# Linear attention and FFN in one kernel: VectorE's prefix sums at the head of the slot, two of GpSimd's steps later, one order of TensorE's last products

## What is computed

```python
q = jnp.exp(split_heads(x @ Wq.T + bq))
k = jnp.exp(split_heads(x @ Wk.T + bk))
v = split_heads(x @ Wv.T + bv)
kv = jnp.cumsum(k[:, :, :, None] * v[:, :, None, :], axis=1)
k1 = jnp.cumsum(k, axis=1)
num = jnp.einsum('zsD,zsDd->zsd', q, kv)
den = jnp.sum(q * k1, axis=-1, keepdims=True)
x = layernorm(x + merge_heads(num / den) @ Wo.T + bo)
h = ((x @ weight) @ aux_weight1) @ aux_weight2
out = layernorm(x + jnp.tanh(h + bias))
```

## Time and profile before

| | |
|---|---|
| median of 3 runs | 2473.36 us |
| the profiled execution | 2476.86 us, span 2473.6 |
| TensorE matmuls | 2267.6 us, 92% of the span |
| TensorE weight loads | 1844.8 us, 75% |
| VectorE | 1935.6 us, 78% |
| GpSimd | 1432.5 us, 58% |
| ScalarE | 990.4 us, 40% |
| granted clock of TensorE, mean | 0.983 |

### The profile page before, as it was taken

One profiled execution on the slowest core, in us unless ns is written; L12 is line 12 of the kernel. 1 busy time (PEld: TensorE's weight loads), 2 busy tenths in 40 slices (PEclk: granted clock), 3 DMA queues, 4 the chain that ended last, 5 costly groups with the idle time before them and its releaser, 6 DMA issues.

```text
span 2473.6 us, 71230 instructions
## 1 busy us (share of the span) xinstructions
PE 2267.6 (92%) x27784; PEld 1844.8 (75%) x27784; DVE 1935.6 (78%) x2316; ACT 990.4 (40%) x1683; POOL 1432.5 (58%) x1925
## 2 busy tenths in 40 slices
PE   4999999999999999999999999999999999999863
PEld 3777777777787777777777777777778777777752
DVE  2578888888888888888888888888888888787753
ACT  2344434444344443444444434444344443443421
POOL 1265666656666566665666656666666666565642
PEclk9999999999999999999999999999999999999987
DMA  6133333333333333332333323333333333332211
GB/s 159 45 104 96 111 95 106 104 100 108 95 108 104 99 104 99 105 107 95 107 100 103 104 95 108 102 102 105 95 105 106 103 104 95 103 106 85 70 44 38
DMA packets 294452, 242.73 MB, mean 98 GB/s; under 512 B 33328, under 2 KB 225840, under 8 KB 294192
## 3 DMA queue, kind: packets, MB, share of 16 engines
q1 hardware_dynamic: 294192, 238.69, 31.2%
HBM read 139.99 MB, written 98.57 MB: 96 GB/s over the span
## 4 chain that ended last, share of the span: by engine, by line
DVE 40%; SPq 17%; issue 13%; DMA 9%; PE 8%; POOL 8%; ACT 5%; POOLq 0%; DVEq 0%; ACTq 0%
DVE WK L689 21%; DMA WK<-x_rows 7%; SPq L277 7%; SPq L284 6%; DVE o L677 4%; DVE k L694 4%; DVE bnst L704 4%; DVE xres L702 3%; ACT WK L524 3%; POOL rstd L770 3%; PE SC L312 2%; SPq L271 2%; PE SC L313 2%; PE SC L314 2%; POOL WK L725 2%
## 5 line engine op out<-in xcount | busy, mean ns | idle before, releaser
L689 DVE TENSOR_TENSOR_SCAN WK<-ones,k,KT 128x128 f32<-128x128 f32 x512 | 557.2, 1147 | 0.0
L677 DVE RECIPROCAL o<-ND 128x512 f32<-128x512 f32 x128 | 428.6, 3348 | 10.7 <-PE ND L419 10.7
L524 ACT ACTIVATE WK<-xres,shift,rstd 128x512 f32<-128x512 f32 x128 | 104.2, 814 | 812.8 <-POOL shift L772 812.8
L745 POOL TENSOR_TENSOR oL<-o,oH 128x512 fp32r<-128x512 f32 x128 | 168.7, 1318 | 274.9 <-ACT oH L544 274.9
L664 DVE BATCH_NORM_STATS2 bnst<-WK 128x6 f32<-128x512 f32 x128 | 88.9, 694 | 299.3 <-POOL WK L725 299.3
L729 POOL TENSOR_SCALAR_AFFINE_SELECT A<-A 128x512 f32<-128x512 f32 x512 | 309.6, 642 | 6.7 <-ACT A L534 6.7
L725 POOL TENSOR_TENSOR WK<-WK 128x512 f32<-128x512 f32 x128 | 163.7, 1279 | 191.3 <-ACT WK L529 191.3
L534 ACT ACTIVATE A<-SC 128x512 f32<-128x512 f32 x512 | 261.8, 594 | 11.8 <-PE SC L410 11.5
L312 PE MATMUL SC<-xTH,WqH 128*128 128x512 f32 x512 | 211.6, 413 | 56.7 <-ACT A L534 28.9
L312 PE MATMUL SC<-WfH,x1H 128*128 128x512 f32 x512 | 205.3, 401 | 45.9 <-POOL x1L L750 24.6
L767 POOL TENSOR_SCALAR ve<-mv 128x1 f32<-128x1 f32 x128 | 28.6, 223 | 351.0 <-DVE mv L706 350.9
(11 more groups left out here) (100 smaller groups left out, 5356.6 us busy)
## 6 DMA issues: line engine op xcount, KB each, us to landing
xin<-x SPq DMA_DIRECT2D x512, 64.0 KB, 2.0
xres<-x SPq DMA_DIRECT2D x128, 256.0 KB, 2.7
x_rows<-WK SPq DMA_DIRECT2D x128, 256.0 KB, 2.3
WK<-x_rows SPq DMA_DIRECT2D x512, 64.0 KB, 2.0
out<-WK SPq DMA_DIRECT2D x128, 256.0 KB, 2.0
k_rows<-WK SPq DMA_DIRECT2D x120, 256.0 KB, 2.5
WK<-k_rows SPq DMA_DIRECT2D x480, 64.0 KB, 1.9
QT<-wqT SPq DMA_DIRECT2D x4, 256.0 KB, 4.7
```

Source lines behind the costliest of these rows:

```text
L524: nc.scalar.activation(x1[:, n % 2, :], xres[:, n % 2, :], ACT.Identity, bias=shift[:, 0:1], scale=rstd[:, 0:1]).then_inc(x1_ready, 1)
L677: nc.vector.reciprocal(o[:, :, :], den_ps).then_inc(recip_ready, 1)
L689: last = nc.vector.tensor_tensor_scan(qk1[:, g, :], ones[:, 0:1].to_broadcast([P, P]), KT[:, s, g, cols], k1[:, k % B, g:g + 1], ALU.mult, ...
```

## The change

VectorE: the four prefix sums, the copy and the product with q (L689 to L697) move from behind the x1s transpose to directly behind L650. The statistics of the second layernorm (L664, L667) move from ahead of the state sum to behind o. GpSimd: the tanh sum (L725) moves from ahead of the masks to behind them; oL (L745) moves from behind the three one-element steps of the second layernorm to ahead of them. TensorE: the FFN is called behind the output projection in every slot, also from 124 on. Nothing is added or taken away; every wait moves with its instruction.

```diff
--- before.py
+++ after.py
@@ -459,11 +459,9 @@
                     wait(pe, scores_out[2], c.count(k + 1))
                     three_pass(v_ps, lambda f: xTH[:, s, f, cols], lambda f: xTL[:, s, f, cols],
                                lambda f: WvH[:, f, :], lambda f: WvL[:, f, :]).then_inc(v_done, 1)
-                if ffn and not proj:
-                    feed_forward()
                 if prev:
                     output_projection()
-                if ffn and proj:
+                if ffn:
                     feed_forward()
 
             run_slots(pe, slot, 8, 2, {-3: multiply_aux, -2: multiply_weight, -1: multiply_bv})
@@ -648,39 +646,6 @@
                     wait(dve, ffn_done, c.count(k - 2))
                     wait(dve, out_stored[(k - 5) % B], c.dma_count(k - 5))
                     nc.vector.tensor_tensor(yf, ffn_ps, bfbc[:, :], ALU.add).then_inc(z_ready, 1)
-                if c.updates_state(k - 1):
-                    wait(dve, k_ready, c.quad_count(k - 1))
-                    wait(dve, ktok_loaded[(k - 2) % B], c.part_count(k - 2))
-                    nc.vector.transpose(KS[:, :].rearrange("p (t g f) -> p g t f", t=HG, f=HD),
-                                        KT[:, ps, :, pcols].rearrange("p g (t q) -> p g t q", q=HD)
-                                        ).then_inc(k_turned, 1)
-                if c.exists(k + 8):
-                    m = k + 8
-                    wait(dve, xin_loaded[m % B], c.part_count(m))
-                    xblocks = xin[:, m % XIN, :]
-                    nc.vector.transpose(xblocks, xblocks).then_inc(x_turned, 1)
-                if fin:
-                    wait(dve, y_ready, c.count(k - 2))
-                    nc.vector.bn_stats(bnst[:, 1, :], yf).then_inc(bn2_ready, 1)
-
-                    wait_before(dve, (bn2_ready, c.count(k - 2)), (shift2_ready, c.count(k - 3)))
-                    nc.vector.bn_aggr(mv2[:, :], bnst[:, 1, :]).then_inc(stats2_ready, 1)
-                if c.updates_state(k - 2):
-                    wait(dve, state_done, c.count(k - 1))
-                    sflat = state[:, (k - 2) % B, :, :].rearrange("p g d -> p (g d)")
-                    nc.vector.tensor_tensor(sflat, state_ps, sflat, ALU.add).then_inc(state_ready, 1)
-                if prev:
-
-                    wait(dve, num_done, c.count(k))
-                    wait(dve, oh_ready, c.count(k - 1))
-                    wait(dve, ol_ready, c.count(k - 1))
-                    nc.vector.reciprocal(o[:, :, :], den_ps).then_inc(recip_ready, 1)
-                    wait(dve, recip_ready, c.count(k))
-                    nc.vector.tensor_tensor(o[:, :, :], num_ps, o[:, :, :], ALU.mult).then_inc(o_ready, 1)
-                if c.exists(k - 2):
-                    n = k - 2
-                    wait(dve, x1s_loaded[n % B], c.part_count(n))
-                    nc.vector.transpose(x1s[:, :], x1s[:, :]).then_inc(x1_turned, 1)
                 if att:
                     wait(dve, k_ready, c.quad_count(k))
                     wait(dve, den_done, c.count(k))
@@ -696,6 +661,39 @@
                     wait(dve, q_ready, c.quad_count(k))
                     nc.vector.tensor_tensor(qk1[:, :, :], qk1[:, :, :], QT[:, s, :, cols],
                                             ALU.mult).then_inc(qk1_ready, 1)
+                if c.updates_state(k - 1):
+                    wait(dve, k_ready, c.quad_count(k - 1))
+                    wait(dve, ktok_loaded[(k - 2) % B], c.part_count(k - 2))
+                    nc.vector.transpose(KS[:, :].rearrange("p (t g f) -> p g t f", t=HG, f=HD),
+                                        KT[:, ps, :, pcols].rearrange("p g (t q) -> p g t q", q=HD)
+                                        ).then_inc(k_turned, 1)
+                if c.exists(k + 8):
+                    m = k + 8
+                    wait(dve, xin_loaded[m % B], c.part_count(m))
+                    xblocks = xin[:, m % XIN, :]
+                    nc.vector.transpose(xblocks, xblocks).then_inc(x_turned, 1)
+                if c.updates_state(k - 2):
+                    wait(dve, state_done, c.count(k - 1))
+                    sflat = state[:, (k - 2) % B, :, :].rearrange("p g d -> p (g d)")
+                    nc.vector.tensor_tensor(sflat, state_ps, sflat, ALU.add).then_inc(state_ready, 1)
+                if prev:
+
+                    wait(dve, num_done, c.count(k))
+                    wait(dve, oh_ready, c.count(k - 1))
+                    wait(dve, ol_ready, c.count(k - 1))
+                    nc.vector.reciprocal(o[:, :, :], den_ps).then_inc(recip_ready, 1)
+                    wait(dve, recip_ready, c.count(k))
+                    nc.vector.tensor_tensor(o[:, :, :], num_ps, o[:, :, :], ALU.mult).then_inc(o_ready, 1)
+                if fin:
+                    wait(dve, y_ready, c.count(k - 2))
+                    nc.vector.bn_stats(bnst[:, 1, :], yf).then_inc(bn2_ready, 1)
+
+                    wait_before(dve, (bn2_ready, c.count(k - 2)), (shift2_ready, c.count(k - 3)))
+                    nc.vector.bn_aggr(mv2[:, :], bnst[:, 1, :]).then_inc(stats2_ready, 1)
+                if c.exists(k - 2):
+                    n = k - 2
+                    wait(dve, x1s_loaded[n % B], c.part_count(n))
+                    nc.vector.transpose(x1s[:, :], x1s[:, :]).then_inc(x1_turned, 1)
                 if prev:
                     wait(dve, oproj_done, c.count(k))
                     wait(dve, xb_ready, c.count(k))
@@ -719,10 +717,6 @@
                 ffn = c.exists(k - 2)
                 fin = c.exists(k - 3)
 
-                if fin:
-                    n = k - 3
-                    wait(pool, tanh_ready, c.count(n + 1))
-                    nc.gpsimd.tensor_tensor(y[:, n % 2, :], y[:, n % 2, :], x1[:, n % 2, :], ALU.add).then_inc(y_ready, 1)
                 if att:
                     for j in range(HG):
                         wait_before(pool, (scores_out[j], c.count(k + 1)))
@@ -730,6 +724,15 @@
                                                        compare_op=ALU.is_ge, fill=0.0, base=0,
                                                        pattern=[[0, NK], [1, P]], channel_multiplier=-1)
                     last.then_inc(masked, 1)
+                if fin:
+                    n = k - 3
+                    wait(pool, tanh_ready, c.count(n + 1))
+                    nc.gpsimd.tensor_tensor(y[:, n % 2, :], y[:, n % 2, :], x1[:, n % 2, :], ALU.add).then_inc(y_ready, 1)
+                if prev:
+                    wait(pool, oh_ready, c.count(k))
+                    wait(pool, oproj_done, c.count(k - 1))
+                    nc.gpsimd.tensor_tensor(oL[:, :, :], o[:, :, :], oH[:, :, :].bitcast(F32),
+                                            ALU.subtract).then_inc(ol_ready, 1)
                 if fin:
                     wait_before(pool, (stats2_ready, c.count(k - 2)))
                     nc.gpsimd.tensor_scalar(ve[:, 1:2], mv2[:, 1:2], EPS, None, ALU.add).then_inc(ve2_ready, 1)
@@ -739,11 +742,6 @@
                     wait_before(pool, (rstd2_ready, c.count(k - 2)))
                     nc.gpsimd.tensor_scalar(shift[:, 1:2], mv2[:, 0:1], rstd[:, 1:2], -1.0, ALU.mult,
                                             ALU.mult).then_inc(shift2_ready, 1)
-                if prev:
-                    wait(pool, oh_ready, c.count(k))
-                    wait(pool, oproj_done, c.count(k - 1))
-                    nc.gpsimd.tensor_tensor(oL[:, :, :], o[:, :, :], oH[:, :, :].bitcast(F32),
-                                            ALU.subtract).then_inc(ol_ready, 1)
                 if ffn:
                     wait(pool, x1h_ready, c.count(k - 1))
                     halves = [t[:, :, :].rearrange("p g (t q) -> p g t q", q=HD) for t in (x1H, x1L)]
```

## The result

After the change the kernel takes 2340.24 us, the median of 4 runs (2339.22 to 2341.11); the kernel before took 2473.22 in the runs beside them (4 runs, 2471.76 to 2480.55). The ratio is 0.9457, with a 95% interval of 0.9438 to 0.9476. The profiled execution took 2341.11 us, span 2339.2, mean granted clock 0.991.

The account below looks back on a forecast made before the run. TensorE's 17.24 us of work a slot plus 0.98 waiting for VectorE, whose scans GpSimd holds. 2476.9 - 98.0 (steady slots) - 20.9 (last slots) - 9.8 (last r) = 2348.2; median 3.5 lower: 2345, range 2318 to 2408.

Parts of the forecast that it names:

- (1): Prefix sums at VectorE's slot head: stage 2.41, reciprocal at 4.6, oL at 9.4, slack before Wo about 1.0 us.
- The price per us: Steady slots: each us of delay beyond the slack before Wo costs 119 us in all.
- (2): VectorE behind o: r no longer queues behind scans, L650 waits only for TensorE, at 0.11; both TensorE waits go.
- (3): SyncE's queue: k_rows store 0.26 later, at about 3.95; x1L ready at 14.0, slack 0.4 before Wf.
- (4): GpSimd's reordered list: tanh-sum waiting vanishes but not as time; xres and xTL to about 16.7, shift at about 0.6.
- (5): Last slots, Wo ahead of Wf: four slots 66 us, -20.9 (-25.7 to -15.3); last r at 13, -9.8.
- The head: Start of the kernel: has its setup and no such wait, so 0 us change.
- (D): Rival for the steady slots: TensorE's wait isn't VectorE's doing, only the tail gains; 2442 us, chance 0.06.
- (B): Rival at shift or x1L: shift meets the scans, or DMA delays x1L; slot 17.9, 2405 us, chance 0.17.
- (C): Rival at the slot's head: scans meet a full-width GpSimd operation; slot 20.2, about 2688 us, chance 0.10.

Follow-up runs that it names:

- the run with the short wait: Kernel after plus a spare VectorE reciprocal of 190 columns (1.25 us) just ahead of the reciprocal before o: 2411.07 us, ratio 0.9738.
- the two waits: Kernel after plus a spare VectorE reciprocal ahead of o, of 190 columns (1.25 us) or 310 (2.03 us): 2411.07 and 2489.20 us.
- The run with 0.8 us added before K: Kernel after plus a spare VectorE reciprocal of 120 columns (0.79 us) ahead of the K and x transposes: 2378.18 us, ratio 0.9626.
- the run with additions at the head: Kernel after plus three two-input GpSimd additions of 320 columns beside the scans at the slot's head: 2521.18 us, ratio 1.0182.
- relieving one neighbour: Kernel before, scans unmoved, GpSimd's addition of constants to xres cut from 512 columns to one: 2371.40 us, ratio 0.9574.

## Why the prediction was right

The time said was 2345 (2318 to 2408), the median is 2340.24. The profiled execution was to take 2348.2 and took 2341.11: 7.0 of the 7.1 are the steady slots; the other errors (-0.6 and +0.4 at the end, +1.6 at the head, -1.4 around the span) cancel, and that is luck. So is part of the median's nearness: I took off 3.5 for it, as in the kernel before, and it is 0.9.

**(1) The stage at the head** was sized rightly: scans 1.61 for 1.57 in the earlier trace rows, the stage 2.54 for 2.41, reciprocal at 4.60 for 4.6, oL at 9.41 for 9.4, Wo at 11.72 for 11.71. The product starts at 2.60, ahead of the masks at 2.97, so its price beside masks isn't paid. The slack, which I put at 1.0, is 0.92 by the run with the short wait: 0.1 passes between oL's end and Wo. The price per us was 119; the two waits give 104 in the medians, and 117 in typical slots (18.39 - 17.65 for 0.75).

**(2) VectorE behind o.** As said: z starts 0.11 after den in all 119 slots; r starts at 14.64, released by TensorE in 88 slots and in the other 31, the slot shown among them, by GpSimd's sum xres, which there ends with Wo.

**(3) SyncE's queue** was mis-sized, on the careful side. The store of k_rows starts at 3.98 for 3.95, but I took the 8.6 from it to x1L as the time of transfers. The earlier trace rows had shown that x1L starts where oL ends, 1217.75 + 1.32 = 1219.07: it was GpSimd's order. In the typical slot now x1L starts at 12.07, right behind the scalars, and is ready at 13.37, about 1.0 ahead of Wf and not 0.4. The run with 0.8 us added before K still waits only 9.1 us before Wf.

**(4) GpSimd's end of the slot** was sized too late. I let xTL run to 16.7 and shift start at 0.6, at the scans' own start. xTL starts at 14.65 in the median slot and ends at 15.94, the scalars wait for VectorE's statistics in most slots and not for xTL, and shift starts at 0.30. For this and (3) I took 17.4 instead of 17.24, and measured was 17.34. That the margin was near in size is luck. Of the 12.0 us above 17.24 a slot, 1.8 are Wq waiting for A behind a late shift, as (4) feared (three slots), and 1.4 are waits before Wf, as (3) did. The other 9 are short stops of TensorE, ahead of Wq with shift and A in time, and within Wq; the prediction has nothing of them.

**(5) The last slots:** -21.5 for -20.9, with the middle value between no cold group and a cold one right in the mean of four slots that are either; the last r at 13.84 for 13. **The head** I put at nothing, by the argument that it had no such wait. It costs 1.6: I had not followed what GpSimd does in the first slots.

**The rivals.** (D) falls: TensorE's order alone gives 0.9917. (B) did not happen. Shift was only a little longer beside scans in the kernel after, as here, where the scans run from 810.58 to 812.19:

```profile
811.03 0.48 POOL L770 TENSOR_SCALAR shift<-mv,rstd 128x1 f32<-128x1 f32 x1 [0.17 <-POOL rstd L768]
```

That is 0.21 more than its 0.27, the most there is in 128 of them. (C)'s mechanism is real: it is what happened in the first slot, in the prefix sums alone, and in the run with additions at the head, which at a stage of 4.95 is 1.8% slower, where I had put the break-even at 4.6. (With the tanh sum first the stage is 3.95 and the time 2410.09; between these two runs the time of before is reached at a stage of about 4.5, by my estimate. The prediction's own terms for (C), 10.7 + 3.74, give Wo at 14.44 and not 14.65, which changes nothing in it.) (C) was not the case here because GpSimd, with its tanh sum moved, has nothing full-width to do between 0 and 2.9. My argument against (C), that masks and tanh sum come later, was too weak by half: masks do, and the tanh sum, at 2.01 in its old place, would have met the copy. It was the change's edit on GpSimd that kept it away. Part (4) of the prediction counted that edit by what it delays, and gave it no gain; and my expectations of the prefix sums alone and of the tanh sum's old place, written later, still missed the copy.

The rule of the Trainium skill ("SBUF — State Buffer", "SBUF: two separate sides"), that an instruction which starts first has the pair of ports to its end, agrees with these rows: the copy of 1.08 and 1.19 us until the tanh sum's end, the turns of scans and additions, and shift's 0.21. What it would have made of (B) is too small to matter, since a one-element step waits for at most one scan.

**What stays open.** The stops of TensorE in the first slot of a round of the loop are 3.6 us in the kernel after and 14.6 with the wait before K, and VectorE's stop of over 4 us behind the loop stands in three runs. These lie in the first slot after a branch back or behind the loop. Others, ahead of Wq in the kernel after, lie mostly in the fifth slot of a round (0.43 us in slot 44). Why, and why some runs have them and others not, no run shows.
```profile
104.55 0.83 DVE L654 TENSOR_TENSOR_SCAN WK<-ones,k,KT 128x128 f32<-128x128 f32 x1
```

That is one scan; what masks would cost beside all four was not tried.

## What to carry to other kernels

When a VectorE instruction with two SBUF inputs is several times as long as its shortest instance, look at what GpSimd runs beside it before moving anything: relieving one neighbour gave nearly all that the whole reorder gave in the steady stretch. Where two engines wait for each other's steps, try the moves of both lists together; each half of this change alone was slower than no change, by 6% and 12%. And cost an edit by what it keeps out of the way too, not only by what it delays.

## What the runs showed of the hardware that I had not expected

A copy of four columns took 1.08 to 1.19 us instead of 0.17, beside a full-width addition on GpSimd: a held instruction of four columns waited like a full-width one. A product group of TensorE that starts after a stop took 2.83 for 2.72 us. And four scans of VectorE against three additions of GpSimd took turns, so that both engines lost: 3.38 for 1.61, and 2.96 for an estimated 2.4. With GpSimd's part alone, TensorE's granted clock fell to 0.50 for part of Wo in 42 slots, after idle time of about 2 us before it, and stayed at the higher level in most slots with the same idle time.
